# A graph attention kernel: who builds block 0's tables and masks, and when the first stage loads the adjacency

## The chip, the cores and the metric

One core of one Trainium2 chip. The kernel is one program with five instruction streams (TensorE, VectorE called DVE, ScalarE called ACT, GpSimd called POOL, and SyncE called SP, which only issues transfers), kept in step by semaphores. The metric is the device time of one execution in microseconds, as the median of several runs.

## The reference

Two layers over a graph of 8192 nodes with 128 features: graph attention with a gated update, then a plain propagation over the adjacency. `adj` holds zeros and ones.

```python
h = jnp.maximum(_layernorm(x), 0.0)
Wh = h @ W;  src = Wh @ a[:F];  dst = Wh @ a[F:]
e = leaky_relu(src + dst.T, 0.2)
att = softmax(where(adj > 0, e, -9e15), axis=1)
h_prime = att @ Wh
gi = h_prime @ w_ih.T + b_ih;  gh = h @ w_hh.T + b_hh     # then the usual gates r, z, n
x = x + (1.0 - z) * n + z * h
h = jnp.maximum(_layernorm(x), 0.0)
x = x + adj @ (h @ W1.T + b1)
```

## The kernel before

The attention is not computed element by element. exp(leaky_relu(s + d)) is a product of a factor of the row and a factor of the column, with one pair of factors where s + d is positive and another where it is negative. So the kernel keeps two tables `TB[:, j, m, :]` (m = 0 and 1) of the features times exp(d) and exp(0.2 d), and for each block of 256 rows two masks in 8-bit floats: `mask1` (an edge, and s + d not negative) and `mask2` (an edge, and negative). The attention is then masks times tables on TensorE. Each table entry is kept as a 16-bit high part and a low part (the rest), side by side, 259 columns in all.

**First stage** (0 to about 50 us). `xb` is loaded in eight parts q of 8 tiles each. For each q, DVE takes the statistics of part q+1 (`stats`: `bn_stats` L569, `bn_aggr` L573), ScalarE takes the square root (`deviation`, L418), DVE the reciprocal (L579) and -mean times it (L581); DVE normalises `BY_DVE` = 6 of the eight tiles in place in `H` (L584), ScalarE the other two (L429). TensorE then transposes four tiles per step k (two steps to a q), ScalarE evacuates them with a Relu into one of four column buffers `hTq[k % 4]` (`column`, L405), TensorE multiplies by the weights (L867) and ScalarE evacuates the result to `WG` (`features`, L411). SP stores each column buffer (L249) and, on odd steps, the rows of `H` (L252). `H` lies in the memory of the masks `M`, so no mask is written before all rows are stored (`p_hout` 128). The column buffers lie in `AE` and `Y[1]`, where DVE later writes products and converted adjacency. Behind steps k = 3 and 7 SP issues the loads of the first two adjacency chunks `X[0]` and `X[1]` (2048 KB each, L255). DVE converts `X[0]` to bytes `Y[0]` (`ones_of`, L617) right after its last normalisation, then waits for the features (L624), and some small steps lead to the first table product.

**Block 0** (g = 0, four chunks c of 16 tiles). The tables are built here, once: for each chunk four pieces i = 4c .. 4c+3 of 8 tiles (even i: first table, odd i: second). DVE forms the product in 32 bits (`table_product`, L653, into `PB[0]` in `AE` or `PB[1]` in `JK`), ScalarE copies it to the high part (`table_high`, L456), and the low part is product minus high: DVE for even i (`table_low`, L658), GpSimd for odd i (L379). Each buffer `PB` is free for the next product when the low part is done. After the tables of a chunk come its comparisons, one for each tile: `first_on_act(0)` = 4, so DVE does 4 (`compare`, L672) and ScalarE 12 (`sign_mask`, L469). Then DVE converts the adjacency of the next chunk (L617) and combines: `mask1` = comparison and adjacency (L680), `mask2` = adjacency xor `mask1` (L684). TensorE does 64 products of a chunk with `mask1`, `mask2` (L894).

**Later blocks** have no tables; DVE does 7 comparisons and ScalarE 9 per chunk, and ScalarE also counts the nonzeros of each adjacency chunk (`count`, L478, which writes its output into `JK`). In block g, after chunk 1, ScalarE evacuates the sums of block g-1 (`evacuate`, L490), without which TensorE can't start block g. Its order from the end of block 0 is: count, 9 masks, count, 9 masks, count, evacuation. GpSimd does one small power per block there (`rstd`, L386).

The order within each engine is written out by hand; an engine that waits holds up all that is behind it.

Of the kernel before, what the change touches and what calls it, by code (L numbers as in the profile page):

```python
# [7 lines left out]
P = 128  # L8
# [16 lines left out]
EPS = 1e-5  # L25
# [3 lines left out]
JC = 16  # L29
# [11 lines left out]
LATE = (NS - 1) * (CS - EARLY) + CS  # L41
BY_DVE = 6

# [24 lines left out]
def binary_adjacency(nc, sem, redo, xb, adjb, w, wt, a, wiht, whht, b_ih, b_hh, w1t, b1, out):  # L68
    ctx = ExitStack()
    with ctx:  # L70
# [113 lines left out]
        p_nd = sem("p_nd")  # L184
        t_p, t_hi, t_lo, t_lop = sem("t_p"), sem("t_hi"), sem("t_lo"), sem("t_lop")
        t_sc = k_w = sem("t_sc")
# [37 lines left out]
        def first_on_act(g):  # L224
            return 4 if isinstance(g, int) and g == 0 else JC - ON_ACT

# [9 lines left out]
        with nc.Block() as block:  # L236
            @block.sync
            def _(sp):
# [8 lines left out]
                for k in range(16):  # L247
                    sp.wait_ge(p_ht, k + 1)
                    sp.dma_start(ht_d[:, k * 512:(k + 1) * 512], hTq[k % 4]).then_inc(p_htout[k % 4], 16)  # L249
                    if k % 2:  # L250
                        q = k // 2
                        sp.dma_start(h_d[:, q * 8:(q + 1) * 8, :], H[:, q * 8:(q + 1) * 8, :]).then_inc(p_hout, 16)  # L252
                    if k in (3, 7):
                        b = k // 4
                        sp.dma_start(X[b][:, :], adjb[b, :, :]).then_inc(c_in[b], 16)  # L255
                    if k == 9:
                        sp.wait_ge(p_bias, 6)
                        for part in range(3):
                            sp.dma_start(b_d[part, :, :], bpart[part]).then_inc(b_in, 16)
                    if k == 13:  # L260
                        sp.wait_ge(b_in, 112)
                        sp.wait_ge(p_one, 1)
                        for part in range(3):
                            sp.dma_start(BI[32 * part:32 * part + 1, :],
                                         b_d[part, :, :].rearrange("r c -> (r c)").rearrange("(o n) -> o n", o=1)).then_inc(
                                             b_in, 16)
# [86 lines left out]
            def _(pool):  # L353
# [8 lines left out]
                                        base=0, pattern=[[-1, P]], channel_multiplier=1).then_inc(p_id, 1)  # L362
                nc.gpsimd.memset(WG[:, :, F + 2:F + 3], 1.0).then_inc(p_one, 1)
                pool.wait_ge(b_in, 64)
                nc.gpsimd.tensor_tensor(brow[0:2, :], brow[0:2, :], bhid, ALU.add).then_inc(p_bias, 1)
                src = [brow] + bres
                for k in range(3):
                    pool.wait_ge(p_bias, 2 * k + 1)
                    nc.gpsimd.tensor_copy(bpart[k], src[k]).then_inc(p_bias, 1)
                    if k < 2:  # L370
                        pool.wait_ge(p_bias, 2 * k + 2)
                        nc.gpsimd.tensor_tensor(bres[k], src[k], bpart[k], ALU.subtract).then_inc(p_bias, 1)
                pool.wait_ge(b_in, 112)
                nc.gpsimd.memset(TB[:, :, :, 2 * TW:2 * TW + 2], 1.0).then_inc(p_one, 1)

                for i in range(1, 16, 2):
                    j = i // 2 * 8
                    pool.wait_ge(t_hi, i + 1)
                    nc.gpsimd.tensor_tensor(TB[:, j:j + 8, 1, TW:2 * TW], PB[1], TB[:, j:j + 8, 1, 0:TW],  # L379
                                            ALU.subtract).then_inc(t_lop, 1)  # L380

# [11 lines left out]
            def _(act):  # L393
# [21 lines left out]

                def deviation(q):
                    act.wait_ge(p_mv, q + 1)
                    nc.scalar.activation(sdx[:, q * 8:(q + 1) * 8],  # L418
                                         mvx[:, q * 8:(q + 1) * 8, 1:2].rearrange("p t k -> p (t k)"), ACT.Sqrt,
                                         bias=epst[:, :]).then_inc(p_sd, 1)  # L420

                act.wait_ge(p_one, 1)
                deviation(0)
                for q in range(8):
                    if q < 7:
                        deviation(q + 1)
                    act.wait_ge(p_nm, q + 1)
# [3 lines left out]
                    ins.then_inc(p_ha, 1)  # L431
                    if q == 7:
                        nc.scalar.activation(wsq[:, :], epst[:, :], ACT.Exp)
                    column(2 * q)
# [23 lines left out]
                def sign_mask(g, u, k, c):  # L458
# [7 lines left out]
                    act.sem_inc(turn, 1)  # L466
                    for jj in range(first_on_act(g), JC):
                        j = c * JC + jj
                        ins = nc.scalar.activation(rows(mask1(c), jj), SB[u][:, :], ACT.Sigmoid, scale=STEEP,  # L469
                                                   bias=dsteep[:, j:j + 1], saturate=False)  # L470
                    ins.then_inc(c_ua, 1)

                def count(g, u, k, c):
                    act.wait_ge(c_in[c % 2], (k * 4 + u * 2 + c // 2 + 1) * 16)
                    if isinstance(g, int) and g == 1 and c == 0:
                        act.wait_ge(t_lop, 8)
                    wait(act, c_cnt, (g - 1) * EARLY + c)
# [36 lines left out]
                def slot(g, u, k):  # L514
# [3 lines left out]
                    for c in range(CS):  # L518
                        if main:
                            if first:  # L520
                                for i in range(4 * c, 4 * c + 4):
                                    table_high(i)
# [42 lines left out]
            def _(dve):  # L565
                def stats(q):
# [5 lines left out]
                    for t in range(q * 8, q * 8 + 8):  # L572
                        ins = nc.vector.bn_aggr(mvx[:, t, :], stx[:, t, :])  # L573
                    ins.then_inc(p_mv, 1)

                def normalised(q):
                    dve.wait_ge(p_sd, q + 1)
                    at = slice(q * 8, q * 8 + 8)
                    nc.vector.reciprocal(rsx[:, at], sdx[:, at]).then_inc(p_rs, 1)  # L579
                    dve.wait_ge(p_rs, q + 1)  # L580
                    nc.vector.scalar_tensor_tensor(nmx[:, at], mvx[:, at, 0:1].rearrange("p t k -> p (t k)"), -1.0,  # L581
# [59 lines left out]
                def table_product(i):  # L641
                    if i == 0:
# [6 lines left out]
                        dve.wait_ge(t_sc, 2)  # L649
                    wait(dve, (t_lo, t_lop)[i % 2], i // 2)  # L650
                    j, m = i // 2 * 8, i % 2
# [9 lines left out]
                def compare(g, u, k, c):  # L661
                    if c == 0:
                        if isinstance(g, int) and g == 0:
                            dve.wait_ge(p_sbe, 1)
                            dve.wait_ge(p_hout, 128)
                        else:
                            dve.wait_ge(s_in[u], (k + u) * 16)
                    wait(dve, c_pe, (g - 1) * CS + c + 1)
# [7 lines left out]
                def combine(g, c):  # L676
                    dve.wait_ge(c_ud, g * CS + c + 1)
                    dve.wait_ge(c_ua, g * CS + c + 1)
# [78 lines left out]
                def slot(g, u, k):  # L757
                    main = in_range(g, 0)
                    first = isinstance(g, int) and g == 0
                    for c in range(CS):  # L760
                        if main:
                            if first:
                                for i in (4 * c, 4 * c + 2):
                                    table_product(i)
                                    table_product(i + 1)
                                    table_low(i)
                            compare(g, u, k, c)
                            if c < CS - 1:
# [87 lines left out]
            def _(pe):  # L856
# [97 lines left out]
                def slot(g, u, k):  # L954
                    for c in range(CS):
                        if isinstance(g, int) and g == 0:
                            pe.wait_ge(t_lo, 2 * (c + 1))
                            pe.wait_ge(t_lop, 2 * (c + 1))
                            if c == 0:
# [728 lines left out]
```

## Time and profile before

| | |
|---|---|
| median of 3 runs | 1615.08 us (1614.78 to 1615.68) |
| the profiled execution | 1614.28 us, its span 1612.7 us |
| TensorE | 1536.0 us busy (95%) |
| DVE | 1138.4 us (71%) |
| ScalarE | 1065.8 us (66%) |
| GpSimd | 44.5 us (3%) |
| TensorE's granted clock, mean | 0.984 |

Times in the profile are microseconds from the start of the span. A row of the timeline gives start, duration, engine, line, operation, output and inputs, and how many equal instructions in a row it merges; in brackets stands idle time of the engine ahead of it and what ended that. Instructions of one engine overlap a little, so the record of one can end after the next has begun.

### The profile page before, as it was taken

To read this page: it belongs to the slowest core of one execution; us is meant where nothing else is said; L and a number is where in the kernel's file an instruction comes from. 1 tells how busy PE (TensorE), PEld (TensorE's weight loads), DVE (VectorE), ACT (ScalarE), POOL (GpSimd) and SP (SyncE) were. 2 spreads that over 40 slices of the span, in tenths; PEclk is the share of its full clock that TensorE was granted. 3 is DMA by queue.
4 is the path that set the end of the run, shared out by engine and by line. 5 is a ranking of instruction groups with operands and counts; after the bars stand their busy time and mean duration, and the time that the engine had idled before them with its cause. 6 is when DMAs were issued, how large, how long until landed. Compare 5 with 4: busy or idle time off the path is not lost.

```text
span 1612.7 us, 34927 instructions
## 1 busy us (share of the span) xinstructions
PE 1536.0 (95%) x13260; PEld 1335.1 (83%) x13260; DVE 1138.4 (71%) x2290; ACT 1065.8 (66%) x1805; POOL 44.5 (3%) x59
## 2 busy tenths in 40 slices
PE   5448999999999999999999999999999999999997
PEld 5336888888888888888888888888888888888887
DVE  8799999999999999999999999999250000000001
ACT  5669999999999999999999999999121000000000
POOL 0220000000000000000000000000000000000000
PEclk9779999999999999999999999999999999999999
DMA  8649999999999999999999999997558444444430
GB/s 330 237 153 348 340 341 338 339 345 336 339 343 339 340 337 344 340 344 338 340 344 341 343 331 341 342 337 283 212 214 357 174 162 159 161 165 176 176 124 15
DMA packets 79955, 454.16 MB, mean 282 GB/s; under 512 B 9176, under 2 KB 38434, under 8 KB 58914
## 3 DMA queue, kind: packets, MB, share of 16 engines
q1 hardware_dynamic: 78322, 444.54, 74.6%
q10 hardware_dynamic: 1584, 8.98, 1.4%
q8 instruction: 28, 0.46, 0.1%
q14 instruction: 21, 0.17, 0.0%
HBM read 369.57 MB, written 83.92 MB: 281 GB/s over the span
## 4 chain that ended last, share of the span: by engine, by line
PE 92%; DVE 5%; DMA 1%; issue 1%; ACT 0%; DVEq 0%; ACTq 0%
PE A L894 56%; PE A L977 28%; PE GP L918 3%; PE GP L919 2%; DMA h_columns<-AE 1%; PE GQ L937 1%; DVE AE L653 1%; PE GP L920 1%; PE GP L917 1%; DVE M L672 1%; DVE JK L653 1%; DVE Y L617 1%; PE TG L904 0%; PE TG L926 0%; DVE JK L569 0%
## 5 line engine op out<-in xcount | busy, mean ns | idle before, releaser
L894 PE MATMUL A<-TB,M 128*128 128x259 f16 x8192 | 940.8, 275 | 47.1 <-DVE M L684 41.1
L894 PEld LDWEIGHTS A<-TB,M 128*128 128x128 fp8e4 x8192 | 797.4, 97 | 174.0 <-issue 48.3
L469 ACT ACTIVATE M<-SB,dsteep 128x256 fp8e4<-128x256 f32 x1164 | 477.5, 502 | 0.0
L478 ACT ACTIVATE JK<-X 128x4096 uint8<-128x4096 uint32 x124 | 448.0, 3613 | 0.0
L617 DVE TENSOR_SCALAR Y<-X 128x4096 fp8e4<-128x4096 f32 x128 | 292.7, 2287 | 3.8 <-DMA X<-in_adjb_dram 3.7
L797 DVE SCALAR_TENSOR_TENSOR hp<-A,R 128x256 f32<-128x256 f32 x32 | 13.6, 425 | 367.5 <-PE A L977 349.0
L672 DVE TENSOR_SCALAR M<-SB,nd 128x256 fp8e4<-128x256 f32 x884 | 250.2, 355 | 0.0
L977 PE MATMUL A<-WG,X 128*128 128x256 f16 x2048 | 225.7, 273 | 0.0
L977 PE MATMUL A<-WG,TB 128*128 128x256 f16 x2048 | 225.2, 273 | 0.0
L977 PEld LDWEIGHTS A<-WG,TB 128*128 128x128 fp8e4 x2048 | 200.4, 98 | 23.2
L977 PEld LDWEIGHTS A<-WG,X 128*128 128x128 fp8e4 x2048 | 200.4, 98 | 23.1
L684 DVE TENSOR_TENSOR M<-Y,M 128x1024 uint32<-128x1024 uint32 x128 | 156.8, 1225 | 4.4
L680 DVE TENSOR_TENSOR M<-M,Y 128x1024 uint32<-128x1024 uint32 x128 | 155.9, 1218 | 0.5 <-issue 0.4
L490 ACT ACTIVATE AE<-A 128x259 f32<-128x259 f32 x128 | 42.0, 383 | 43.3 <-PE A L894 43.3
L918 PE MATMUL GP<-wihT,hpT 128*128 128x384 f32 x128 | 51.7, 486 | 0.0
L386 POOL TENSOR_TENSOR rstd<-ve,half 128x2 f32<-128x2 f32 x32 | 22.9, 716 | 1041.8 <-DVE ve L741 1041.8
L919 PEld LDWEIGHTS GP<-whhT,R 128*128 128x128 f32 x128 | 24.3, 190 | 17.0
L919 PE MATMUL GP<-whhT,R 128*128 128x256 f32 x128 | 38.1, 379 | 0.0
L689 DVE TENSOR_TENSOR AE<-AE 128x516 f32<-128x516 f32 x32 | 22.4, 699 | 21.8 <-ACT AE L490 21.6
L920 PEld LDWEIGHTS GP<-whhT,R 128*128 128x128 f32 x128 | 24.3, 190 | 3.3
L918 PEld LDWEIGHTS GP<-wihT,hpT 128*128 128x128 f32 x128 | 24.3, 190 | 2.4
L556 ACT ACTIVATE JK<-M 128x4096 uint8<-128x4096 uint32 x4 | 14.5, 3617 | 17.9 <-DMA M<-in_adjb_dram 17.9
(133 smaller groups left out, 696.8 us busy)
## 6 DMA issues: line engine op xcount, KB each, us to landing
X<-in_adjb_dram SPq DMA_DIRECT2D x128, 2048.0 KB, 9.5
mask_bytes<-Y SPq DMA_DIRECT2D x128, 512.0 KB, 4.7
X<-mask_bytes SPq DMA_DIRECT2D x16, 2048.0 KB, 9.3
TB<-mask_bytes SPq DMA_DIRECT2D x16, 2048.0 KB, 9.2
M<-in_adjb_dram ACTq DMA_DIRECT2D x4, 2048.0 KB, 10.2
M<-in_xb_dram SPq DMA_DIRECT2D x8, 512.0 KB, 8.5
h_rows<-M SPq DMA_DIRECT2D x8, 512.0 KB, 6.6
R<-in_xb_dram SPq DMA_DIRECT2D x32, 128.0 KB, 6.8
```

Of the source, the lines that this page charges most:

```text
L469: ins = nc.scalar.activation(rows(mask1(c), jj), SB[u][:, :], ACT.Sigmoid, scale=STEEP, bias=dsteep[:, j:j + 1], saturate=False)
L478: nc.scalar.activation(junk, X[c % 2][:, :].bitcast(u32), ACT.Sign, accum_out=nz[:, bass.ts(g, 1), c:c + 1].rearrange("p g c -> p (g c)")) ...
L490: ins = nc.scalar.activation(AE[:, 2 * t + m, 0:2 * TW + 1], A[t][m][:, 0:2 * TW + 1], ACT.Copy)
L617: nc.vector.tensor_scalar(Y[c % 2][:, :].bitcast(f8), X[c % 2][:, :], 1.0, MARK, ALU.is_equal, ALU.mult, saturate=False).then_inc(c_y, 1)
L672: ins = nc.vector.tensor_scalar(rows(mask1(c), jj), SB[u][:, :], nd[:, j:j + 1], None, ALU.is_ge, saturate=False)
L680: nc.vector.tensor_tensor(mask1(c), mask1(c), Y[c % 2][:, :], ALU.bitwise_and).then_inc(c_m1, 1)
L684: nc.vector.tensor_tensor(mask2(c), Y[c % 2][:, :], mask1(c), ALU.bitwise_xor).then_inc(c_m2, 1)
L894: ins = nc.tensor.matmul(A[t][m][:, 0:2 * TW + 1], rows((mask1, mask2)[m](c), jj)[:, t * P:(t + 1) * P], TB[:, c * JC + jj, m, 0:2 * TW + ...
L918: nc.tensor.matmul(bank[:, 0:3 * F], a_t, wihT[:, :], start=False, stop=False)
L919: nc.tensor.matmul(bank[:, 0:2 * F], h_t, whhT[:, 0:2 * F], start=False, stop=False)
L920: ins = nc.tensor.matmul(bank[:, 3 * F:4 * F], h_t, whhT[:, 2 * F:3 * F], start=False, stop=True)
L977: ins = nc.tensor.matmul(PH2[b][:, d * 2 * F:(d + 1) * 2 * F], YB[b][:, j * RW + d * P:j * RW + (d + 1) * P], GS[:, j, :], start=(d == 0 a ...
```

## The change

In words:
- Block 0: all low parts are done by DVE, in the order product, product, low, low; GpSimd's part and its semaphore `t_lop` are gone. All sixteen comparisons of a chunk are ScalarE's; it does the copies of a chunk's last two pieces between the eighth and the ninth of them. DVE does none in block 0.
- First stage: DVE adds epsilon to the variance, GpSimd raises it to the power -0.5 for eight tiles at once (four of these ahead of its work on the biases, four behind), in place of ScalarE's square root and DVE's reciprocal. ScalarE's table for exponentials is loaded at the start. `BY_DVE` is 5, so ScalarE normalises three tiles of eight.
- The loads of the first two adjacency chunks are issued behind steps 11 and 15.

```diff
-BY_DVE = 6
+BY_DVE = 5
         def first_on_act(g):
-            return 4 if isinstance(g, int) and g == 0 else JC - ON_ACT
+            return 0 if isinstance(g, int) and g == 0 else JC - ON_ACT
...
-                    if k in (3, 7):
-                        b = k // 4
+                    if k in (11, 15):
+                        b = k // 4 - 2
                         sp.dma_start(X[b][:, :], adjb[b, :, :]).then_inc(c_in[b], 16)
...
+                def deviation(q):
+                    pool.wait_ge(p_sd, q + 1)
+                    at = slice(q * 8, q * 8 + 8)
+                    nc.gpsimd.tensor_tensor(rsx[:, at], sdx[:, at], half[:, 0:1].to_broadcast([P, 8]), ALU.pow).then_inc(
+                        p_rs, 1)
+
+                for q in range(4):
+                    deviation(q)
                 pool.wait_ge(b_in, 64)
...
+                for q in range(4, 8):
+                    deviation(q)
                 pool.wait_ge(b_in, 112)
                 nc.gpsimd.memset(TB[:, :, :, 2 * TW:2 * TW + 2], 1.0).then_inc(p_one, 1)
-
-                for i in range(1, 16, 2):
-                    j = i // 2 * 8
-                    pool.wait_ge(t_hi, i + 1)
-                    nc.gpsimd.tensor_tensor(TB[:, j:j + 8, 1, TW:2 * TW], PB[1], TB[:, j:j + 8, 1, 0:TW],
-                                            ALU.subtract).then_inc(t_lop, 1)
...
-                def deviation(q):
-                    act.wait_ge(p_mv, q + 1)
-                    nc.scalar.activation(sdx[:, q * 8:(q + 1) * 8],
-                                         mvx[:, q * 8:(q + 1) * 8, 1:2].rearrange("p t k -> p (t k)"), ACT.Sqrt,
-                                         bias=epst[:, :]).then_inc(p_sd, 1)
-
                 act.wait_ge(p_one, 1)
-                deviation(0)
+                nc.scalar.activation(wsq[:, :], epst[:, :], ACT.Exp)
                 for q in range(8):
-                    if q < 7:
-                        deviation(q + 1)
...
-                    if q == 7:
-                        nc.scalar.activation(wsq[:, :], epst[:, :], ACT.Exp)
...
                     for jj in range(first_on_act(g), JC):
+                        if isinstance(g, int) and g == 0 and jj == JC // 2:
+                            for i in range(4 * c + 2, 4 * c + 4):
+                                table_high(i)
...
-                        act.wait_ge(t_lop, 8)
+                        act.wait_ge(t_lo, 16)
...
-                                for i in range(4 * c, 4 * c + 4):
+                                for i in range(4 * c, 4 * c + 2):
                                     table_high(i)
...
+                    dve.wait_ge(p_mv, q + 1)
+                    nc.vector.tensor_scalar(sdx[:, q * 8:(q + 1) * 8],
+                                            mvx[:, q * 8:(q + 1) * 8, 1:2].rearrange("p t k -> p (t k)"), EPS, None,
+                                            ALU.add).then_inc(p_sd, 1)
 
                 def normalised(q):
-                    dve.wait_ge(p_sd, q + 1)
+                    dve.wait_ge(p_rs, q + 1)
                     at = slice(q * 8, q * 8 + 8)
-                    nc.vector.reciprocal(rsx[:, at], sdx[:, at]).then_inc(p_rs, 1)
-                    dve.wait_ge(p_rs, q + 1)
...
-                    wait(dve, (t_lo, t_lop)[i % 2], i // 2)
+                    wait(dve, t_lo, i - 1)
...
                                     table_product(i)
                                     table_product(i + 1)
                                     table_low(i)
-                            compare(g, u, k, c)
+                                    table_low(i + 1)
+                            else:
+                                compare(g, u, k, c)
...
-                            pe.wait_ge(t_lo, 2 * (c + 1))
-                            pe.wait_ge(t_lop, 2 * (c + 1))
+                            pe.wait_ge(t_lo, 4 * (c + 1))
```

## Rows read from the trace of the kernel before

**Rows 1.** The page's costliest groups: count, busy and mean, idle before, releaser.

```profile
L894 PE MATMUL A<-TB,M 128*128 128x259 f16 x8192 | 940.8, 275 | 47.1 <-DVE M L684 41.1
```

**Rows 2.** Timeline of TensorE, the last batch of block 0 and the restart.

```profile
120.03 9.57 PE L894 MATMUL A<-TB,M 128*128 128x259 f16 x64 [7.19 <-DVE M L684]
135.57 8.66 PE L894 MATMUL A<-TB,M 128*128 128x259 f16 x64 [5.96 <-issue]
```

**Rows 3.** Timeline of ScalarE, chunk 3 of block 0 to the evacuation.

```profile
105.61 1.07 ACT L456 ACTIVATE TB<-JK 128x1032 f16<-128x1032 f32 x1
...
111.11 1.07 ACT L456 ACTIVATE TB<-JK 128x1032 f16<-128x1032 f32 x1
112.08 4.87 ACT L469 ACTIVATE M<-SB,dsteep 128x256 fp8e4<-128x256 f32 x12
116.86 3.60 ACT L478 ACTIVATE JK<-X 128x4096 uint8<-128x4096 uint32 x1
...
134.85 1.16 ACT L490 ACTIVATE AE<-A 128x259 f32<-128x259 f32 x4
```

**Rows 4.** Timeline of DVE, chunk 3 of block 0.

```profile
103.20 1.23 DVE L653 TENSOR_TENSOR AE<-WG,bt 128x1032 f32<-128x1032 f32 x1
...
105.57 1.24 DVE L658 TENSOR_TENSOR TB<-AE,TB 128x1032 f16<-128x1032 f32 x1
106.84 3.09 DVE L653 TENSOR_TENSOR AE<-WG,bt 128x1032 f32<-128x1032 f32 x1
...
112.22 2.96 DVE L672 TENSOR_SCALAR M<-SB,nd 128x256 fp8e4<-128x256 f32 x4
115.10 2.28 DVE L617 TENSOR_SCALAR Y<-X 128x4096 fp8e4<-128x4096 f32 x1
...
118.55 1.22 DVE L684 TENSOR_TENSOR M<-Y,M 128x1024 uint32<-128x1024 uint32 x1
119.69 1.92 DVE L672 TENSOR_SCALAR M<-SB,nd 128x256 fp8e4<-128x256 f32 x7
```

**Rows 5.** Timeline of GpSimd: last work on the biases, one of eight subtractions.

```profile
19.47 0.28 POOL L369 CAST TB<-TB 5x128 bf16<-5x128 f32 x1
...
106.76 2.08 POOL L379 TENSOR_TENSOR TB<-JK,TB 128x1032 f16<-128x1032 f32 x1 [8.74 <-ACT TB L456]
```

**Rows 6.** Timeline of DVE, first stage: two normalisations, the first step behind the features, the first product.

```profile
27.18 1.62 DVE L584 TENSOR_SCALAR M<-M,JK 128x128 f32<-128x128 f32 x6
...
31.24 1.62 DVE L584 TENSOR_SCALAR M<-M,JK 128x128 f32<-128x128 f32 x6
...
50.89 0.26 DVE L624 TENSOR_REDUCE bad<-WG 128x1 f32<-128x64 f32 x1 [8.29 <-ACT WG L411]
...
53.67 1.23 DVE L653 TENSOR_TENSOR AE<-WG,bt 128x1032 f32<-128x1032 f32 x1
```

**Rows 7.** Timeline of ScalarE, first stage: the columns of step 5 and 8, two normalisations.

```profile
21.57 0.60 ACT L405 ACTIVATE AE<-GQ 128x512 f32<-128x512 f32 x1
...
31.68 0.60 ACT L405 ACTIVATE AE<-TG 128x512 f32<-128x512 f32 x1 [3.50 <-DMA h_columns<-AE]
...
34.75 0.86 ACT L429 ACTIVATE M<-M,JK 128x128 f32<-128x128 f32 x2
...
38.32 0.86 ACT L429 ACTIVATE M<-M,JK 128x128 f32<-128x128 f32 x2
```

**Rows 8.** Adjacency loads, issue to landing: L255 (first two), then L301 (126 later).

```profile
DMA to landing us min/median/max: 10.0/12.2/14.3
...
DMA to landing us min/median/max: 7.4/9.5/10.8
```

**Rows 9.** A power on GpSimd and DVE beside it; the page's group of the latter.

```profile
300.74 0.69 POOL L386 TENSOR_TENSOR rstd<-ve,half 128x2 f32<-128x2 f32 x1 [32.23 <-DVE ve L741]
300.81 0.70 DVE L689 TENSOR_TENSOR AE<-AE 128x516 f32<-128x516 f32 x1
...
L689 DVE TENSOR_TENSOR AE<-AE 128x516 f32<-128x516 f32 x32 | 22.4, 699 | 21.8 <-ACT AE L490 21.6
```

More of the change, by code:

```diff
@@ L184, in binary_adjacency @@
         p_nd = sem("p_nd")
-        t_p, t_hi, t_lo, t_lop = sem("t_p"), sem("t_hi"), sem("t_lo"), sem("t_lop")
+        t_p, t_hi, t_lo = sem("t_p"), sem("t_hi"), sem("t_lo")
         t_sc = k_w = sem("t_sc")
@@ L363, in _ @@
                 nc.gpsimd.memset(WG[:, :, F + 2:F + 3], 1.0).then_inc(p_one, 1)
+                pool.wait_ge(p_one, 1)
+                def deviation(q):
[5 more added lines that the diff above has]
+                    deviation(q)
                 pool.wait_ge(b_in, 64)
@@ L662, in compare @@
                     if c == 0:
[L663 to L667, printed above, removed]
+                        dve.wait_ge(s_in[u], (k + u) * 16)
                     wait(dve, c_pe, (g - 1) * CS + c + 1)
@@ L676, in combine @@
                 def combine(g, c):
-                    dve.wait_ge(c_ud, g * CS + c + 1)
+                    wait(dve, c_ud, (g - 1) * CS + c + 1)
                     dve.wait_ge(c_ua, g * CS + c + 1)
```

## The prediction, made before the changed kernel ran

> **What bounds the kernel now.** I read the page first. TensorE is the bound nearly everywhere, and the row of its main products says where it is not: it stands idle for 47.1 us ahead of them, 41.1 us of that waiting for the second mask [rows 1]. The timeline of TensorE puts nearly all of this ahead of 135.57 us: block 0 gets a batch of 64 products only every 16.5 us, the last one at 120.03, and then there is a gap of 5.96 us before the batch at 135.57, from which TensorE runs without a break to the end of the main part [rows 2]. So a change of the first 135 us is worth exactly what it moves that restart; from there on the sum of TensorE's work stands, about 1,477 us.
>
> What sets the restart? It needs ScalarE's evacuation of block 0's sums at 134.85. ScalarE reaches it 17.99 us after its last block 0 mask, at 116.86, and has no gap between (three counts and two sets of nine comparisons come first, all in its order) [rows 3]. DVE has long had the masks ready. So the restart follows ScalarE's last mask of block 0, and that follows DVE, which feeds it products. I therefore count two things: when DVE's first product starts (53.67), and how long block 0 takes from there to ScalarE's last mask.
>
> **Block 0, chunk by chunk.** I take chunk 3; the others repeat it. DVE goes from 103.20 to 119.69 = 16.49 us [rows 4]. Two of its steps are stretched: a product of 3.09 us where the same product elsewhere has 1.23, while the GpSimd subtraction at 106.76 runs (2.08), and four comparisons in 2.96 us, which at the spacing of the seven at 119.69, 0.26, would be about 1.1 [rows 4, 5]. The change removes both GpSimd subtractions and all four comparisons and adds two subtractions to DVE (1.23 each, at most 1.27 from start to start).
>
> With 0 as the start of the first product, the new chunk goes: products at 0 and 1.2; first low half at 2.37 (when ScalarE's copy is ready, as now); second at 3.62, its copy (105.61 + 1.07 = 3.48) being ready; products 3 and 4 at 4.8 and 6.0, done at 7.1. ScalarE: second copy at 2.41, masks from 3.38 (as far behind as 112.08 is behind 111.11), eight at (4.87 - 0.49)/11 = 0.40 us = 3.2, so the third copy starts at 6.56 and is done at 7.63. So DVE waits 0.5 us for it; low halves at 7.66 and 8.91, conversion of the adjacency at 10.1, the two combines after it, for which I keep the present distances (115.10 to 118.55 is 3.45, then 1.14), end at 14.7. ScalarE's fourth copy starts at 7.53, the other eight masks go from 8.5 to 11.7, in time for the combine at 12.3 [rows 3, 4]. A chunk is 14.7 instead of 16.5: 1.8 us, three times until the last chunk starts, 5.4 us. In the last chunk ScalarE is done at 11.7 instead of 116.86 - 103.20 = 13.66: 2.0 us more. **Block 0: 7.4 us earlier.** ScalarE's first count now waits for the last low half, done at 10.1, which is earlier than its turn, so this costs nothing; it would cost if the low halves slipped by 1.6 us. ScalarE's four comparisons more, 1.6 us, are in the 11.7.
>
> **First stage.** Three edits meet here.
>
> (a) DVE. Its period, from one set of six normalisations to the next, is 31.24 - 27.18 = 4.06 us [rows 6]. One of six goes to ScalarE, (1.62 - 0.34)/5 = 0.26; the reciprocal goes, an addition of the same size comes. New period 3.80. ScalarE's own period, where it was catching up, is 38.32 - 34.75 = 3.57 [rows 7]; it loses its square root, gains a normalisation of 0.39, and stays near 3.8 as well.
>
> (b) The loads. The two 2048 KB adjacency loads go behind the column stores of steps 11 and 15 instead of 3 and 7. Today ScalarE waits 3.50 us ahead of 31.68, and once more later, for an old column store before it may overwrite its buffer [rows 7]. A period now stores 1024 KB; since even 2048 KB land in 7.4 us, half of it fits a period of 3.8, so I take both waits as gone. What comes in its place is the load itself: DVE's order puts the first conversion of the adjacency ahead of everything that leads to the tables. The first load is issued behind step 11. Step 5 ends now at 22.1 (21.57 + 0.6); two periods at 0.26 less give 21.5, three more periods 33.0, and some 0.5 for the small work that DVE has in the middle, 33.5. The column and row stores are issued first, about 1.2, so the load is issued at 34.7. Loads of this size land in 7.4 to 10.8 us later in the kernel (median 9.5), in 10.0 and 14.3 in this stage [rows 8]; the queue ahead holds only 768 KB, so I take 9.5: 44.2. The conversion takes 2.2: 46.4. Columns and features would be done by 33.5 + 2 x 3.8 + 2 = 43.1, so the load decides, by 3 us. From there to the first product it is 53.67 - 50.89 = 2.78 us as now, when DVE sits idle for 8.29 us ahead of 50.89 [rows 6], so 49.2 instead of 53.67: **4.5 us earlier**. The removed load of ScalarE's table for exponentials late in the stage lies inside the 3 us and adds nothing.
>
> Behind the moved loads stand the stores of steps 12 to 15, the row stores that all masks wait for, the second adjacency load and the small store of the scores. The bytes behind the first load (2 MB of stores, 2 MB of load) need 5 to 6 us each: the stores are down at 50, where the masks want them at 52.6, the second adjacency half at 55, where it is wanted at 59.
>
> (c) The powers on GpSimd. The trace has no power of eight elements, only one of two, 0.69 us [rows 9]. It costs between 0.69 (nothing per element) and 4 x 0.69 = 2.76. Each is asked for one period (3.8) before DVE needs it, so as a wait it is hidden at either price; the first has only 2.2 us, which costs at most 0.6. Powers 4 to 7 stand in GpSimd's order behind the bias work, which ends at 19.75 [rows 5]; power 4 is asked for at 21. Behind power 7 stands the filling of the tables' ones, wanted only at 50. The question is whether DVE stands still meanwhile, as it did for the subtraction. Each power runs just when DVE normalises. Here the trace has a direct answer: at 300.74 a power runs over a DVE addition of two SBUF operands that starts at 300.81, and this takes 0.70 us, the mean of all 32 of them (699 ns), though most of it lies beside the power [rows 9]. So a power holds DVE up for next to nothing. Bounds: 0 and 2.76 per period; I take 0, for the row is of the same instruction.
>
> The Trainium skill speaks against this (SBUF — State Buffer, Who interferes with whom): whichever of a GpSimd instruction and a contending VectorE instruction starts first has the shared ports for its whole length, and the other blocks. The trace agrees for the subtraction and not for the power; by the rule the time would be that of the second rival below.
>
> **Sum.** -7.4 - 4.5 = -11.9 us. The profiled execution had 1614.28 (span 1612.7 and 1.6 around it), which becomes 1602.4; the median is 0.8 higher, so **1603.2 us**.
>
> **Rivals.**
> First, the late adjacency load lands as slowly as the slow one of this stage, 14.3 us instead of 9.5: the first stage gains nothing, 4.8 us more than forecast, 1608.0. Against it: no other adjacency load is near. Chance 0.10.
>
> Second, powers block DVE. At 0.69 each, six of them ahead of the load, 4.1 us: 1607.3. At 1.7, in the middle, 10 us: 1613.4. For it: GpSimd's subtraction did block. Against: the power at 300.74, though the DVE operation there is another one than the normalisation. Chance 0.14 below 1.4 us each, 0.05 above.
>
> Third, slower than before: the same place, but a power of eight costs four times that of two, 2.76, and holds DVE all the time: 16.6 us lost, less 11.9, 1619.8. It decides from (11.9 + 3.2)/6 = 2.5 us lost in each period. Chance 0.04.
>
> Fourth, the change of block 0 does not reach the restart whole: ScalarE's last 2.0 us are lost since counts or DVE's own masks of block 1 become what is late, 1605.2. Against: DVE waits for the evacuation today. Chance 0.09.
>
> The forecast has 0.53, between 1600.5 and 1604.8 (a landing of 7.4 to 10.8, and the 0.5 us wait in each chunk there or not). The remaining 0.05 is a larger gain. From 1600.5 to 1609.5 lie the forecast, the first and fourth rival and the cheap end of the second. A change under 0.2% (3.2 us) can't be told from none here; the dear end of the second rival gives that, 0.07 with the borders. Faster 0.88, slower 0.05.
>
> **What would show it.** First product of the tables at about 49; chunks 14.7 us apart, no product over 1.3 us on DVE; ScalarE's evacuation and TensorE's restart at 123.7, after which nothing differs. DVE's six, now five, normalisations at 1.4 us in all say that powers don't block; 3 or more say they do. The conversion ahead of the tables should wait for its load. Wrong it would be, above all, if the normalisations are stretched, or if that load lands after 47.

## The result, and the profile after

The changed kernel takes 1602.37 us (median of 4, 1601.63 to 1602.88) against 1615.38 us in the runs of before that were made with it: a ratio of 0.992, 95% interval 0.9905 to 0.9935. The forecast was 1603.2, from 1600.5 to 1609.5. The profiled execution took 1601.98 us with a span of 1600.4, against 1614.28 and 1612.7 before: 12.3 us less, where 11.9 were worked out.

The page's group of main products, then the timeline of TensorE (they answer to [rows 1, 2]):

```profile
L893 PE MATMUL A<-TB,M 128*128 128x259 f16 x8192 | 942.4, 275 | 37.8 <-DVE M L681 31.9
```

```profile
107.67 9.72 PE L893 MATMUL A<-TB,M 128*128 128x259 f16 x64 [4.40 <-DVE M L681]
123.31 8.76 PE L893 MATMUL A<-TB,M 128*128 128x259 f16 x64 [5.92 <-issue]
```

The restart is at 123.31 instead of 135.57, 12.26 us earlier. From it to the end of the span there are 1477.1 us in both kernels, so nothing else is in the result. The gap ahead of the restart is as long as before (5.92 against 5.96).

First stage, timeline of DVE (answers to [rows 6]):

```profile
29.95 1.36 DVE L585 TENSOR_SCALAR M<-M,JK 128x128 f32<-128x128 f32 x5
...
33.73 1.37 DVE L585 TENSOR_SCALAR M<-M,JK 128x128 f32<-128x128 f32 x5
35.60 0.17 DVE L582 SCALAR_TENSOR_TENSOR JK<-JK 128x8 f32<-128x8 f32 x1 [0.50 <-POOL JK L369]
...
44.23 2.29 DVE L618 TENSOR_SCALAR Y<-X 128x4096 fp8e4<-128x4096 f32 x1 [7.18 <-DMA X<-in_adjb_dram]
46.44 0.26 DVE L625 TENSOR_REDUCE bad<-WG 128x1 f32<-128x64 f32 x1
...
49.20 1.23 DVE L654 TENSOR_TENSOR AE<-WG,bt 128x1032 f32<-128x1032 f32 x1
```

The same stretch on GpSimd, and the chain of work that ended last where it passes the first adjacency load:

```profile
30.04 1.74 POOL L369 TENSOR_TENSOR JK<-JK,half 128x8 f32<-128x8 f32 x1 [2.05 <-DVE JK L575]
33.82 1.74 POOL L369 TENSOR_TENSOR JK<-JK,half 128x8 f32<-128x8 f32 x1 [2.05 <-DVE JK L575]
```

```profile
34.96 9.12 DMA X<-in_adjb_dram
```

Three things are to be seen. The period of DVE is 33.73 - 29.95 = 3.78. A power of eight elements takes 1.74 us (30.04 to 31.78), the five normalisations (29.95 to 31.31) lie nearly whole beside it, and these take 1.36 to 1.37, which is their length at the old spacing (1.43 in the one period where GpSimd also works on the biases, at 21.71). And DVE then sits idle for 7.18 us until the load is down: the load, not the features, decides (these are done at 42.50), and first product and load are where the sum had them (49.20 against 49.2, issue 34.96 against 34.7, 9.12 us of landing against 9.5).

Block 0, chunk 3, timeline of DVE and of ScalarE (they answer to [rows 4] and [rows 3]):

```profile
92.93 1.23 DVE L654 TENSOR_TENSOR AE<-WG,bt 128x1032 f32<-128x1032 f32 x1
...
95.30 1.24 DVE L659 TENSOR_TENSOR TB<-AE,TB 128x1032 f16<-128x1032 f32 x1
...
97.59 1.23 DVE L654 TENSOR_TENSOR AE<-WG,bt 128x1032 f32<-128x1032 f32 x1
...
100.59 1.23 DVE L659 TENSOR_TENSOR TB<-AE,TB 128x1032 f16<-128x1032 f32 x1 [0.62 <-ACT TB L452]
...
106.34 1.23 DVE L681 TENSOR_TENSOR M<-Y,M 128x1024 uint32<-128x1024 uint32 x1
107.48 1.92 DVE L669 TENSOR_SCALAR M<-SB,nd 128x256 fp8e4<-128x256 f32 x7
```

```profile
101.41 3.28 ACT L468 ACTIVATE M<-SB,dsteep 128x256 fp8e4<-128x256 f32 x8
104.60 3.60 ACT L477 ACTIVATE JK<-X 128x4096 uint8<-128x4096 uint32 x1
...
122.58 1.17 ACT L489 ACTIVATE AE<-A 128x259 f32<-128x259 f32 x4
```

The chunk takes 107.48 - 92.93 = 14.55 us (16.49 before), no product is over 1.23, and the one wait is 0.62 us for ScalarE's third copy. ScalarE is done 104.60 - 92.93 = 11.67 us after the chunk's first product, and 17.98 us later it evacuates, as before.

### The profile page after: what moved, and what is told of

It reads as the page before. It is cut to its first block, busy times and chain, and to the rows that moved or that the text cites. A ratio compares the mean times of both kernels' runs of the same rounds, so it can differ in the third digit from the quotient of the medians.

```text
span 1600.4 us, 34919 instructions
## 1 busy us (share of the span) xinstructions
PE 1534.7 (96%) x13260; PEld 1333.3 (83%) x13260; DVE 1125.8 (70%) x2274; ACT 1071.0 (67%) x1820; POOL 40.5 (3%) x59
## 4 chain that ended last, share of the span: by engine, by line
PE 93%; DVE 4%; ACT 1%; issue 1%; DMA 1%; SPq 0%; DVEq 0%
PE A L893 56%; PE A L975 28%; PE GP L917 3%; PE GP L918 2%; PE GQ L936 1%; PE GP L919 1%; PE GP L916 1%; ACT M L468 1%; DVE Y L618 1%; DVE JK L568 1%; DMA X<-in_adjb_dram 1%; DVE M L585 0%; PE TG L903 0%; PE TG L925 0%; DVE M L681 0%
## 5 line engine op out<-in xcount | busy, mean ns | idle before, releaser
L468 ACT ACTIVATE M<-SB,dsteep 128x256 fp8e4<-128x256 f32 x1180 | 484.5, 504 | 0.0
L669 DVE TENSOR_SCALAR M<-SB,nd 128x256 fp8e4<-128x256 f32 x868 | 238.4, 349 | 0.0
```

The lines of the kernel that those rows point to most:

```text
L669: ins = nc.vector.tensor_scalar(rows(mask1(c), jj), SB[u][:, :], nd[:, j:j + 1], None, ALU.is_ge, saturate=False)
```

## The experiments

The number read first in each is the first table product on DVE and the restart on TensorE. Only f2 and f3 were timed four times. The others ran once: such a time is good to about a microsecond, and the marks in the trace decide. The marks vary too: two pairs of kernels with the same first stage (before and e1, the changed kernel and e8) differ by 0.5 and 0.3 us in the first product. "The changed kernel" has 49.20 and 123.31, the kernel before 53.67 and 135.57.

**e1, block 0 part alone**, on the kernel before: all edits of `t_lop`, `table_high`, `table_low`, `first_on_act`, `compare`; nothing of the first stage.

```diff
-                    wait(dve, (t_lo, t_lop)[i % 2], i // 2)
+                    wait(dve, t_lo, i - 1)
...
-            return 4 if isinstance(g, int) and g == 0 else JC - ON_ACT
+            return 0 if isinstance(g, int) and g == 0 else JC - ON_ACT
```

> Only the block 0 part of the change, on the kernel before. My account: the first product stays at 53.7, a chunk takes 14.55 us instead of 16.5, and ScalarE's last mask comes 7.4 to 7.8 us earlier; restart of TensorE at about 127.9, 1606.7 us. Rival (this part and the first stage overlap, since both draw on the same slack): restart above 130. Rival (the block 0 part is all of the gain): restart near 123.3.

First product 54.16, restart 128.26: 74.10 us between them, as in the changed kernel (74.11), against 81.90 before. So block 0 is shorter by 7.8 us by itself. The time is 1608.54 us against 1614.29 of the kernel before beside it, only 5.75 less: the first product came 0.5 later, and 1.3 are gone again behind the restart (1478.4 us to the end of the span instead of 1477.1), where the first batch takes 10.19 us instead of 8.66.

**e2, first stage alone**: `BY_DVE`, the loads and the powers; GpSimd's subtractions and DVE's comparisons stay.

```diff
-BY_DVE = 6
+BY_DVE = 5
...
-                    if k in (3, 7):
-                        b = k // 4
+                    if k in (11, 15):
+                        b = k // 4 - 2
```

> Only the first-stage part, with block 0 as before (GpSimd's subtractions and four comparisons of DVE per chunk are back). My account: first product at 49.2, chunks of 16.5 us, restart at about 131.1, 1609.8 us. Rival (the late first load gains nothing by itself): first product at 53 or later.

First product 50.61, restart 132.49 (81.88 us between them, the old length), 1613.02 us against 1614.29 beside it. So the length of block 0 does not depend on the first stage; the two parts share no slack. The first product is 1.4 us later than expected although the load was issued earlier, as the chain of work shows:

```profile
34.42 11.05 DMA X<-in_adjb_dram
```

In the eight other kernels with the load behind step 11 it took 9.0 to 9.5. What makes that difference is open. The time is 3.2 us above the expected 1609.8: 1.4 of it are this, 0.9 lie behind the restart (its first batch takes 9.83 us), and the rest lies outside the span. Alone, then, the first stage moved the restart by only 3.1 us; its 4.5 us are seen where the load lands in 9.1.

**e3, loads early again**, on the changed kernel.

```diff
-                    if k in (11, 15):
-                        b = k // 4 - 2
+                    if k in (3, 7):
+                        b = k // 4
```

> The changed kernel with the two adjacency loads back behind steps 3 and 7. My account: ScalarE waits again for old column stores, about 3 us twice; features end at about 49, first product at about 52, restart at about 126, 1605 us. Rival (powers on GpSimd and the moved table load make the gain of the stage, not the late loads): first product at 49 or earlier.

First product 52.53, restart 126.64, 1606.36 us. Its timeline of ScalarE has both waits back:

```profile
31.96 0.60 ACT L411 ACTIVATE AE<-TG 128x512 f32<-128x512 f32 x1 [4.76 <-DMA h_columns<-AE]
...
42.22 0.60 ACT L411 ACTIVATE AE<-TG 128x512 f32<-128x512 f32 x1 [2.56 <-DMA h_columns<-AE]
```

The same step of the kernel before:

```profile
42.25 0.60 ACT L405 ACTIVATE AE<-TG 128x512 f32<-128x512 f32 x1 [3.06 <-DMA h_columns<-AE]
```

So with the rest of the stage in place the late loads are worth 3.3 us. With the loads early, the rest is worth 1.1. It arises behind the second wait, which ends at the same time in both; the table load of 1.28 us, which stood there before (at 46.20), is the nearest candidate, not shown by a run of its own. These two figures are not shares of the 4.5: e6 shows what the rest is worth once the loads are late.

**e4, the first load behind step 9** (after the small bias stores), on the changed kernel.

```diff
-                    if k in (11, 15):
-                        b = k // 4 - 2
...
+                    if k in (9, 15):
+                        b = k // 15
```

> The changed kernel with the first adjacency load behind step 9 instead of 11. My account: the load was 3 to 4 us later than the features, so it now lands at about 41, the conversion is done at 43, first product at about 46, restart at about 120.3, 1599 us. Rival: the load stands ahead of the stores of steps 10 and 11 and ScalarE waits for them; then the features end after 46 and nothing is gained.

The rival won. Timeline of DVE, then of ScalarE:

```profile
40.52 2.29 DVE L618 TENSOR_SCALAR Y<-X 128x4096 fp8e4<-128x4096 f32 x1 [3.70 <-DMA X<-in_adjb_dram]
...
45.98 0.26 DVE L625 TENSOR_REDUCE bad<-WG 128x1 f32<-128x64 f32 x1 [3.16 <-ACT WG L417]
```

```profile
41.18 0.60 ACT L411 ACTIVATE Y<-TG 128x512 f32<-128x512 f32 x1 [2.05 <-DMA h_columns<-Y]
```

The load was down by 40.5, but ScalarE stood 2.05 us for a column store behind it, and the features ended 3.4 us later. The wait itself is only part of that. TensorE stood still meanwhile, and its next 16 products, first here and then in the changed kernel, are 1.5 us slower:

```profile
41.83 3.69 PE L866 MATMUL A<-wext,Y 128*128 128x130 f32 x16 [1.98 <-ACT Y L411]
```

```profile
39.91 2.17 PE L866 MATMUL A<-wext,Y 128*128 128x130 f32 x16
```

The granted clock is 0.58 from 41.5 to 43.5 and 0.65 from 43.5 to 46, mostly the lower level of 1.2 GHz, after 1.00 before the wait; in the changed kernel it is 0.99 to 1.00 in this stretch. First product 48.76, restart 122.86, 1601.93 us: no difference that one run can tell. An earlier load only moves the wait from DVE to ScalarE.

**e5, a stream beside the normalisations**: the subtraction's output is not used.

```diff
+                    if q > 0:
+                        nc.gpsimd.tensor_tensor(
+                            TBf[:, 16384 + q * 2048:16384 + q * 2048 + 1680].bitcast(f32).rearrange("p (j f) -> p j f", f=120),
+                            ones[:, 0:120].rearrange("p (o f) -> p o f", o=1).to_broadcast([P, 7, 120]),
+                            ones[:, 0:120].rearrange("p (o f) -> p o f", o=1).to_broadcast([P, 7, 120]), ALU.subtract)
                     nc.gpsimd.tensor_tensor(rsx[:, at], sdx[:, at], half[:, 0:1].to_broadcast([P, 8]), ALU.pow).then_inc(
```

> The changed kernel, with one more GpSimd instruction ahead of each power but the first: a subtraction of 840 elements (about 1.7 us, the length of a power of eight) whose output is not used. My account: such a stream holds DVE up where a power of the same length does not; DVE's five normalisations take about 2.9 us instead of 1.4 in each of seven periods, the first adjacency load is issued 8 to 10 us later, restart near 132. Rival (the normalisation shares nothing with GpSimd, so no instruction of GpSimd can hold it up): normalisations stay at 1.4 us, only the powers come later, restart before 126.

Timeline of GpSimd, and of DVE beside it:

```profile
31.36 1.69 POOL L370 TENSOR_TENSOR TB<-ones 128x840 f32<-128x840 f32 x1 [2.36 <-DVE JK L581]
33.02 1.63 POOL L374 TENSOR_TENSOR JK<-JK,half 128x8 f32<-128x8 f32 x1
```

```profile
31.27 2.63 DVE L591 TENSOR_SCALAR M<-M,JK 128x128 f32<-128x128 f32 x5
```

The same five normalisations take 2.63 us beside a subtraction of 1.69, and 1.36 beside a power of 1.74. Within the five it can be seen where: the second starts at 31.52, the third only at 33.06, when the subtraction (31.36 to 33.05) is done, and the last three take 0.85 us, their length at the old spacing, although a power runs from 33.02. The load was issued at 43.86, 8.9 us later, first product 58.36, restart 132.46, 1612.23 us. So the normalisation can be held up from GpSimd, and a power of the same length does not do it.

**e6, square roots and reciprocals back**, with the late table load, on the changed kernel.

```diff
-                    nc.gpsimd.tensor_tensor(rsx[:, at], sdx[:, at], half[:, 0:1].to_broadcast([P, 8]), ALU.pow).then_inc(
...
+                    nc.vector.reciprocal(rsx[:, at], sdx[:, at]).then_inc(p_rs, 1)
```

> The changed kernel with ScalarE's square roots and DVE's reciprocals back in place of the powers; the table for exponentials is loaded late again. My account: periods of 3.9 instead of 3.8, the table load lies beside the wait for the adjacency, first product at most 1 us later, restart at about 124, 1602.9 us. Rival (the powers carry the gain of the stage): first product at 52 or later.

First product 49.11, restart 123.21, 1601.97 us. The powers and the early table load gain nothing here: the load decides, and it is issued at 34.68 against 34.96 with the powers. So late loads and three tiles on ScalarE give the whole of the stage's 4.5 us.

**e7, evacuation first**, on the changed kernel.

```diff
+                        if isinstance(g, int) and g == 1 and c == 1:
+                            evacuate(g - 1)
                         if main:
                             if c + 1 < EARLY:
...
-                        if c == 1 and in_range(g, 1):
+                        if c == 1 and in_range(g, 1) and not (isinstance(g, int) and g == 1):
```

> The changed kernel, with ScalarE's evacuation of block 0 ahead of its third count of block 1 instead of behind it. My account: TensorE's gap of 5.9 us ahead of the restart is ScalarE's order alone; the evacuation comes at 119.0, restart at 119.7, and since ScalarE is two chunks ahead nothing of it is lost, 1598.4 us. Rival: ScalarE's lead is used up and TensorE waits for masks later in blocks 1 and 2, total near 1602.

Restart 119.47, 1599.39 us. The mark is where it was expected, the time 1 us above: TensorE has one more gap, of 0.80 us, a little later, and the batch at the restart is 0.2 longer than in the changed kernel.

```profile
119.47 8.97 PE L895 MATMUL A<-TB,M 128*128 128x259 f16 x64 [1.95 <-issue]
...
153.97 7.32 PE L895 MATMUL A<-TB,M 128*128 128x259 f16 x64 [0.80 <-issue]
```

**e8, conversion in the gap**, on the changed kernel.

```diff
                                     table_product(i + 1)
+                                    if i % 4:
+                                        ones_after(g, u, k, c)
                                     table_low(i)
                                     table_low(i + 1)
...
+                            if not first:
+                                ones_after(g, u, k, c)
```

> The changed kernel, with DVE's conversion of the next adjacency chunk in block 0 between the fourth product and the third low part, where DVE waits 0.6 us for ScalarE's copy. My account: chunks of 14.0 instead of 14.55 us, nothing in the last chunk, restart 1.7 us earlier, 1600.3 us. Rival: the combine then waits for ScalarE's masks or the last low part delays the first count, and nothing is gained.

`ones_after` is the conversion that stood behind the low parts. The chunks take 14.2 us, where 14.0 were expected, restart 121.92, of which 0.3 is an earlier first product (48.88). 1601.45 us, where 1600.3 were expected: the restart is 1.4 us earlier, and 0.9 of it is gone again behind it; the batch at the restart takes 9.64 us instead of 8.76 (more on that in the last section).

**g1, six normalisations on DVE**, on the changed kernel (`BY_DVE = 6`).

> The changed kernel with six normalisations on DVE again instead of five. My account: DVE's period sets when the first adjacency load is issued: 4.05 instead of 3.80, load issued at about 36.3 instead of 35.0, first product at 50.6, restart at 124.7, 1603.4 us. Rival (ScalarE sets the period): nothing changes, or it is faster.

DVE's period is 4.04, as expected, but the load is issued at 35.45, only 0.5 us later than in the changed kernel and not 1.3, first product 49.67, restart 123.76, 1604.59 us at a span of 1601.6. The chain of work that ended last, where it leaves DVE for TensorE, ScalarE and SP, first in the changed kernel, then here:

```profile
30.03 1.04 DVE M L585 x4
...
33.13 0.61 ACT Y L411
...
34.16 0.76 SPq L252
```

```profile
30.84 1.04 DVE M L585 x4
...
33.95 0.61 ACT Y L411
...
34.98 0.43 SPq L252
```

In both kernels the chain is DVE's up to its set of normalisations for steps 10 and 11, and the column of step 11 comes exactly as much later (0.82) as that set (0.81). So it is DVE that sets the issue, and the rival, ScalarE, is not borne out. The set is 0.81 later and not 1.3, since DVE's first set starts 0.22 earlier here, and since two of the changed kernel's five periods, while GpSimd works on the biases, are longer by 0.2 in all. Another 0.33 comes from SP, which takes 0.43 us for the row store ahead of the load and not 0.76.

**f2, the first conversion late**: e7 and e8, and the first conversion not ahead of the tables.

```diff
-                ones_of(0, 0, 0, 0)
...
                                     if i % 4:
+                                        if c == 0:
+                                            ones_of(0, 0, 0, 0)
```

> The changed kernel with three edits together: the first conversion of the adjacency no longer ahead of the steps that lead to the tables but in the first chunk, where DVE waits for ScalarE's copy; the other conversions of block 0 in that gap too; the evacuation of block 0 ahead of ScalarE's third count. My account: the features end at 42.5, so the first product comes at 45.3 instead of 49.2; the first chunk takes 16.3 us, the next 14.2 each; restart near 116.8 instead of 123.3, of which 1 to 1.5 us are given back by the clock and by a later wait: 1597 us. Rival: column or row stores, queued behind the first adjacency load, hold the first product or the masks up, and it is no better than 1600.

Timeline of DVE, then of TensorE:

```profile
45.28 1.23 DVE L655 TENSOR_TENSOR AE<-WG,bt 128x1032 f32<-128x1032 f32 x1 [0.24 <-DMA h_columns<-AE]
...
52.24 2.29 DVE L620 TENSOR_SCALAR Y<-X 128x4096 fp8e4<-128x4096 f32 x1
```

```profile
116.57 7.32 PE L903 MATMUL A<-TB,M 128*128 128x259 f16 x64 [3.43 <-issue]
```

1596.60 us (1596.35 to 1597.60), 0.9885 of the kernel before, interval 0.9868 to 0.9901: 5.8 us below the changed kernel. The step from which the first product hangs is now the features, but for the 0.24 us.

No run has the late conversion alone, but the marks divide the 6.74 us by which the restart is earlier: the first product 3.92, less 1.48 for a longer first chunk (16.11 us); 0.70 in the two chunks behind it; 3.60 from there to the restart, by the order of the evacuation (in e7 it is 3.62 from first product to restart). Of the 6.74, 1.0 is given back behind the restart: its first batch is 1.4 shorter than in the changed kernel, but there are two gaps that the changed kernel does not have:

```profile
131.97 0.81 PE L927 MATMUL GP<-wihT,hpT 128*128 128x384 f32 x2 [0.70 <-ACT hpT L503]
...
151.07 7.32 PE L903 MATMUL A<-TB,M 128*128 128x259 f16 x64 [1.80 <-issue]
```

**f3, the same with the load behind step 13.**

```diff
-                    if k in (11, 15):
-                        b = k // 4 - 2
+                    if k in (13, 15):
+                        b = (k - 13) // 2
```

> As the one before, with the first adjacency load behind step 13 instead of 11, since it is wanted only at 52 now. My account: the stores of steps 12 and 13 land earlier, the load at about 49, in time; the same time as the one before within 1 us, or up to 1 us less if the stores were what the first product waited for. Rival: the load comes too late for the conversion in the first chunk, first chunk above 17 us.

1596.37 us (1596.26 to 1596.81), ratio 0.9881, interval 0.9865 to 0.9898: the same as f2. First product 45.25; the masks of the first chunk wait 1.98 us for the row stores instead of 0.68, and the restart is at 117.14, 0.6 later, which the totals do not show. Neither of the two can be called the better one; they are the best versions here.

**f4, f2 with the square roots.** The edit is that of e6.

> The version with the late first conversion (first adjacency load behind step 11), with ScalarE's square roots and the late load of the table for exponentials back in place of the powers. My account: in the changed kernel these lay beside the wait for the adjacency load; here the features decide, so the table load (1.28 us) and a little of the square roots show: first product at 46.6 to 47.5 instead of 45.28, restart at 118 to 118.9. Rival (the powers are worth nothing here either): first product at 45.3.

First product 47.28, restart 118.55, 1598.34 us. Now that the features decide, the powers and the early table load are worth 2.0 us. Most of it is the table load: ScalarE starts its last normalisations 0.6 us later than in f2 (38.55 against 37.96) and the column behind them, with the table load in between, 2.1 us later (41.22 against 39.12).

## Why the prediction was right

**Block 0, 7.4 us.** Right in mechanism and size: 14.55 us a chunk against 14.7, 11.67 to ScalarE's last mask against 11.7, 7.8 us in all (e1). The sum was 0.4 short, 0.14 in each of three chunks: it had 2.44 us from the third low half to the conversion (7.66 to 10.1), and DVE needs 2.30 (100.59 to 102.89). That the wait for the third copy would be there (0.5 worked out, 0.62 measured) came from laying ScalarE's eight masks beside DVE's products. The fourth rival did not happen: the 17.98 us from last mask to evacuation are unchanged.

**First stage, 4.5 us.** 4.47 measured. That the load would take the place of the removed waits, and decide by some 3 us, is shown by DVE's 7.18 us of idle time and by e6, where nothing that ends before the load matters. The features ended at 42.5, 3.9 us ahead of the conversion's end, where I had 3.3. That DVE's period sets the time of the issue was right too: the chain of work in the changed kernel and in g1 is DVE's up to the last set before it. What was luck is the landing: I took the median of later loads, 9.5, without a load of this place to go by; it took 9.12, and 11.05 in e2, where the same edits gave 3.1 us and not 4.5.

**The restart as the only mark.** I wrote that a change of the first 135 us is worth exactly what it moves the restart. It is so here (1477.1 us behind it in both), but not in general: in nine of the twelve other kernels there are 0.9 to 1.4 us more behind it. That the batch at the restart takes 8.76 us where it took 8.66 was not foreseen and is luck; in other kernels here it takes 7.32 to 10.19.

**Powers.** The term taken, nothing, was right. The reason given, a power of two elements beside another operation, was thin; e5 against the changed kernel is what separates a power from a stream of the same length. The unknown duration was 1.74 us, between the bounds of 0.69 and 2.76. The rule of the Trainium skill on the shared ports (SBUF — State Buffer, Who interferes with whom), by which whichever instruction starts first has them for its whole length, fits the subtraction in e5 and not the power. One statement was wrong: not every power is asked for a period ahead. Behind the last statistics no others stand, so the last power is asked for only 1.4 us before, and DVE waited 0.50 us for it; that cost nothing only because DVE then waited for the load anyway.

**What I did not see.** The forecast named DVE's order, conversion ahead of the tables, as the new bound, and did not ask what that order is worth. f2 shows 5.8 us with two more edits of order; the late conversion has 2.4 us of its restart (3.92 less 1.48).

**Open.** Why the load landed in 11.1 us in e2. And e4 and e8 ran once: their times alone don't tell them from the changed kernel.

## What to carry to other kernels

Find the one mark from which everything shifts as a block (here TensorE's restart), and price a change by what it moves that mark, but look behind it as well, for a microsecond can be lost there. Two parts that lie in series on the way to it add up by their own lengths: 7.8 for block 0 in e1, 4.5 for the first stage. The parts run alone did not add up: e1 and e2 moved the restart by 7.3 and 3.1 us, both together by 12.3, for the same first stage came out 0.5 us later in e1 than before, and 1.4 later in e2 than in the changed kernel. When a wait for a transfer is cured by issuing another one later, work out when that other one lands and what is queued behind it in the hand-written order: the wait moved from ScalarE's buffers to DVE's first conversion, issuing earlier only moved it back (and TensorE, idle meanwhile, went on at the lower clock), and what helped was to let the consumer come later. An improvement that lies beside a longer wait (the powers and the early table load) is worth nothing until that wait is gone, and should be timed again then.

## What the runs showed of the hardware

A power on GpSimd takes 0.69 us for two elements in each partition (median of the 32 in the kernel before; the longest 1.08) and 1.64 to 1.74 for eight. DVE's normalisations beside the latter are not held up: the longest of the 40 in the changed kernel took 0.41 us, most 0.34, and five in a row 1.36 to 1.43 in all. A subtraction that streams 840 elements in 1.69 us lengthens the five by 1.3 us, and the longest single one in e5 took 1.97 us.

The clock at the restart. The stretch of the restart batch in four kernels (the columns are its bounds and length, the busy time of TensorE, its weight loads, DVE, ScalarE and GpSimd with instruction counts, granted clock, share of the DMA engines, GB/s): the kernel before, the changed one, e1 and f2.

```profile
135.57:144.20 8.63, 8.63 (x66) 7.01 (x67) 8.02 (x18) 8.63 (x16) 0.00 (x0) 0.84 0.99 381
```

```profile
123.31:132.07 8.76, 8.76 (x66) 7.11 (x67) 8.15 (x18) 8.76 (x17) 0.00 (x0) 0.83 0.99 395
```

```profile
128.26:138.45 10.19, 10.19 (x66) 7.86 (x67) 9.58 (x23) 10.19 (x20) 0.00 (x0) 0.71 1.01 386
```

```profile
116.57:123.90 7.33, 7.33 (x66) 6.38 (x67) 6.97 (x18) 7.33 (x13) 0.00 (x0) 1.00 0.95 333
```

The same 64 products take from 7.33 us, wholly at the upper level of 2.4 GHz, to 10.19, of which more than half is at 1.2 GHz (mean 0.71). TensorE had been idle for 3.4 to 6.1 us before, and had worked in batches with gaps of 4 to 8 us before that. The gap right before does not order them: e7 has the shortest, 1.95 us, and its batch takes 8.97. What each batch got changes from kernel to kernel by up to 2.9 us, without any edit to TensorE's products; what decides it is not shown. This is one reason why two kernels whose restart differs by a microsecond can't be ranked by their total.
